# Channel-normalised pixels kept in their natural order: the permutation moves from ScalarE's operands to TensorE's PSUM writes, and one subtraction moves from VectorE to GpSimd

## The reference

```python
corrs = [jnp.sum(x * jax.lax.dynamic_slice(xp, (0, 0, di, dj), (b, c, h, w)), axis=1) for di in range(k) for dj in range(k)]
gs = gs / norm
feat = jnp.concatenate([x, gs], axis=1)
out = jnp.einsum('bchw,oc->bohw', feat, W) + bias[None, :, None, None]
return jax.nn.relu(out)
...
return frac_b * b_out + frac_s * s_out + x
...
x = x + _L0_conv_ref(_gn(x), L0_conv_W, L0_conv_bias)
x = x + _L1_conv_ref(_gn(x), L1_conv_w1, L1_conv_b1, L1_conv_w2, L1_conv_b2)
```

## Time and profile before

| | |
|---|---|
| median of 3 runs | 4609.29 us (4605.99 to 4613.17) |
| the profiled execution | 4614.89 us, its span 4613.1 us |
| TensorE busy | 3847.0 us (83%) |
| VectorE busy | 3520.3 us (76%) |
| ScalarE busy | 2589.7 us (56%) |
| GpSimd busy | 637.1 us (14%) |
| mean granted TensorE clock | 0.928 of full speed |

### The profile page before, as it was taken

How to read it: one execution, slowest core, us unless ns; L and a number is a source line. 1 busy time by engine, 2 the same in 40 slices (tenths; PEclk the granted TensorE clock), 3 DMA queues, 4 the chain that set the end, 5 groups by cost and what they waited for, 6 DMA issues and landing times. The chain is left out here.

```text
span 4613.1 us, 73329 instructions
## 1 busy us (share of the span) xinstructions
PE 3847.0 (83%) x23656; PEld 2135.8 (46%) x23657; DVE 3520.3 (76%) x4010; ACT 2589.7 (56%) x2830; POOL 637.1 (14%) x624
## 2 busy tenths in 40 slices
PE   3999999999999999999989767898888777777665
PEld 2655555555555555555556443343333333323222
DVE  5676667667666765766665576899999999999994
ACT  4777777777777777777777434443333233232322
POOL 0000000000000000000000012333232322222221
PEclk9999999999999999999999878898899888888887
DMA  4233322323333232333321246553333333323221
GB/s 167 97 116 116 109 103 100 134 98 116 116 116 111 99 120 97 116 116 116 115 98 61 61 129 217 180 182 154 146 147 134 132 143 125 134 107 123 111 119 48
DMA packets 174313, 556.98 MB, mean 121 GB/s; under 512 B 91248, under 2 KB 91248, under 8 KB 157552
## 3 DMA queue, kind: packets, MB, share of 16 engines
q1 hardware_dynamic: 152016, 283.62, 17.7%
q0 software_dynamic: 21920, 268.59, 15.1%
HBM read 277.23 MB, written 274.86 MB: 120 GB/s over the span
## 5 line engine op out<-in xcount | busy, mean ns | idle before, releaser
L931 DVE TENSOR_TENSOR arena<-arena 128x2048 f32<-128x2048 f32 (+4 forms) x730 | 1759.1, 2430 | 107.7 <-ACT arena L579 66.3
L1250 PE MATMUL psum<-arena 128*128 128x512 f32 x1072 | 615.0, 658 | 442.0 <-issue 399.0
L1056 PE MATMUL psum<-arena 128*128 128x256 f16 (+1 forms) x6344 | 744.2, 272 | 152.7 <-DVE arena L713 134.8
L579 ACT ACTIVATE arena<-arena 128x4096 f32<-128x4096 f32 x67 | 244.2, 3645 | 972.3 <-DVE arena L931 706.6
L1079 PE MATMUL psum<-arena 128*128 128x512 f16 x2048 | 782.3, 382 | 0.7 <-ACT arena L520 0.7
L1080 PE MATMUL psum<-arena 128*128 128x512 f16 x2048 | 782.3, 382 | 0.0
L1081 PE MATMUL psum<-arena 128*128 128x512 f16 x2048 | 782.1, 382 | 0.0
L520 ACT ACTIVATE arena<-psum,bias_sb 128x512 f32<-128x512 f32 x512 | 577.5, 1184 | 270.6 <-PE psum L1134 171.3
L1056 PEld LDWEIGHTS psum<-arena 128*128 128x128 f16 x6344 | 597.4, 99 | 241.5 <-issue 124.1
L713 DVE TENSOR_TENSOR arena<-arena 128x512 f16<-128x512 f32 x512 | 351.7, 687 | 432.0 <-ACT arena L508 431.9
L506 ACT ACTIVATE arena<-arena,gbias,grstd 128x512 f32 (+1 forms) x512 | 669.3, 1307 | 6.0 <-DVE arena L713 4.7
(11 more groups left out here) (138 smaller groups left out, 2672.0 us busy)
## 6 DMA issues: line engine op xcount, KB each, us to landing
arena<-in_x SPq DMA_DIRECT2D x64, 2048.0 KB, 12.6
y_planes<-arena SPq DMA_DIRECT2D x64, 2048.0 KB, 7.9
arena<-arena SPq DMA_DIRECT2D x1536, 8.0 KB, 1.7
arena<-plane_records,arena POOLq DMA_INDIRECT x67, 3.0
arena<-y_planes,arena POOLq DMA_INDIRECT x67, 9.4
out<-arena POOLq DMA_INDIRECT x67, 8.7
arena<-in_wt SPq DMA_DIRECT2D x1, 1024.0 KB, 12.6
cst<-in_consts SPq DMA_DIRECT2D x1, 768.0 KB, 4.3
```

The source lines that it names most:

```text
L931: ins = dve.tensor_tensor(dst, a, b, ALU.max)
L1056: return pe.matmul(dst, w, m, start=(k == 0), stop=(k == nk - 1))
L1250: pe.matmul(dst, diag[:, s, 0, :], bufs[:, u, b * CW:(b + 1) * CW], start=True, stop=False)
```

## The change

`normalise` reads x and writes `g32` and `gh` in natural order, and `conv_out` reads and writes natural order. All operands of these ScalarE instructions become contiguous. The Gram matmuls take natural-order pixels and put their columns into class order through the access pattern of their PSUM output (`classed`, which now iterates natural order over class-order storage). Consecutive columns are 16 float32 (64 bytes) apart there. The transposes write PSUM through the same pattern. The tail writes into a natural-order convolution bank, with consecutive columns 8 float32 apart instead of in runs of 16 neighbours. The constants `band` and `pick` are adapted, and the partitions of a Gram block are now in natural order. The low parts are formed on GpSimd, after its two small instructions of the same chunk, with the same semaphores. VectorE keeps the statistics of the next image in one piece.

```diff
-        def turned(a):
-            return a.rearrange("p (u r j k) -> p u k r j", r=2, j=8, k=8)
         def classed(a):
-            return a.rearrange("p (u k r j) -> p u k r j", k=8, r=2, j=8)
+            return a.rearrange("p (u k r j) -> p u r j k", k=8, r=2, j=8)
...
         @block.gpsimd
+            def low_parts(i, c):
+                n0 = (i * CH + c) * CT
+                slot = slice((c % RING) * CW, (c % RING + 1) * CW)
+                for ct in range(CT):
+                    pool.wait_ge(s_gh, n0 + ct + 1)
+                    pool.tensor_tensor(gl[:, ct, slot], g32[:, ct % 2, :], gh[:, ct, slot],
+                                       ALU.subtract).then_inc(s_gl, 1)
+            def image(i, last):
                 for c in range(CH):
...
                     pool.tensor_tensor(fl[:, half, :], fn, fh[:, half, :], ALU.subtract).then_inc(s_t, 1)
+                    if c + 3 < CH:
+                        low_parts(i, c + 3)
+                    elif not last:
+                        low_parts(i + 1, c + 3 - CH)
...
-                    piece = turned(xs(ct, c * CW, CW, i % 2))
-                    act.activation(classed(g32[:, ct % 2, :]), piece, ACT.Identity, bias=gbias[:, ct:ct + 1],
+                    piece = xs(ct, c * CW, CW, i % 2)
+                    act.activation(g32[:, ct % 2, :], piece, ACT.Identity, bias=gbias[:, ct:ct + 1],
                                    scale=grstd[:, ct:ct + 1])
-                    act.activation(classed(gh[:, ct, (c % RING) * CW:(c % RING + 1) * CW]), piece, ACT.Identity,
+                    act.activation(gh[:, ct, (c % RING) * CW:(c % RING + 1) * CW], piece, ACT.Identity,
...
-                act.activation(turned(relu[:, o % 2, :]), classed(psum[:, o, :]), ACT.Relu, bias=bias_sb[:, o:o + 1],
+                act.activation(relu[:, o % 2, :], psum[:, o, :], ACT.Relu, bias=bias_sb[:, o:o + 1],
...
-            def low_parts(i, c, stats=None):
-                n0 = (i * CH + c) * CT
-                slot = slice((c % RING) * CW, (c % RING + 1) * CW)
-                for ct in range(CT):
-                    dve.wait_ge(s_gh, n0 + ct + 1)
-                    dve.tensor_tensor(gl[:, ct, slot], g32[:, ct % 2, :], gh[:, ct, slot],
-                                      ALU.subtract).then_inc(s_gl, 1)
-                    if stats:
-                        stats(ct)
...
-                        low_parts(i, c + 3, (lambda ct: x_stats(i + 1, c, ct)) if c < 4 and not last else None)
-                    elif not last:
-                        low_parts(i + 1, c + 3 - CH)
+                    if c < 4 and not last:
+                        for ct in range(CT):
+                            x_stats(i + 1, c, ct)
...
-                        dst = psum[:, GRAM0 + t % 2, col:col + n]
+                        dst = classed(psum[:, GRAM0 + t % 2, col:col + n])
...
-                    last = pe.transpose(psum[:, BANK_N, (t % PAIRS) * P:(t % PAIRS + 1) * P],
+                    last = pe.transpose(classed(psum[:, BANK_N, (t % PAIRS) * P:(t % PAIRS + 1) * P]),
...
-                src = tpair[0:REP, half, :].rearrange("p (t q u s) -> p q u t s", t=QUADS, q=2, u=PAIRS)
+                src = tpair[0:REP, half, :].rearrange("p (t q s) -> p q t s", t=QUADS, q=2)
-                    dst = psum[:, o, :].rearrange("p (u t q s) -> p q u t s", u=PAIRS, t=QUADS, q=2)
+                    dst = psum[:, o, :].rearrange("p (s t q) -> p q t s", t=QUADS, q=2)
```

More of the change, by code:

```diff
@@ L49, in const_arrays @@
     p = np.arange(P)
-    k, r, j = p // 16, p // 8 % 2, p % 8
-    w = 8 * j + k
-    band = (np.abs(w[:, None] - w[None, :]) <= KS // 2).astype(np.float32)
+    w_col = 8 * (p % 8) + p // 16
+    band = (np.abs(p[:, None] % W - w_col[None, :]) <= KS // 2).astype(np.float32)
     pick = np.zeros((P, 3, 2, QUADS, 32), np.float32)
     for role in range(3):
+        r, k = (p // 8 % 2, p // 16) if role == AFTER else (p // W, p % 8)
         for e in range(2):
@@ L400, in _ @@
         def _(pool):
-            def image(i):
+            def low_parts(i, c):
[6 more added lines that the diff above has]
+            def image(i, last):
                 for c in range(CH):
@@ L411, in image @@
                     pool.tensor_tensor(fl[:, half, :], fn, fh[:, half, :], ALU.subtract).then_inc(s_t, 1)
-            image(0)
-            with pool.Fori(1, B) as i:
-                image(i)
+                    if c + 3 < CH:
+                        low_parts(i, c + 3)
+                    elif not last:
+                        low_parts(i + 1, c + 3 - CH)
+            for c in range(3):
+                low_parts(0, c)
+            image(0, False)
+            with pool.Fori(1, B - 1) as i:
+                image(i, False)
+            image(B - 1, True)
             pool.wait_ge(s_conv, B * CH * CT)
@@ L777, in image @@
                         keep_stats(i - 1)
-                    if c + 3 < CH:
-                        low_parts(i, c + 3, (lambda ct: x_stats(i + 1, c, ct)) if c < 4 and not last else None)
-                    elif not last:
-                        low_parts(i + 1, c + 3 - CH)
+                    if c < 4 and not last:
+                        for ct in range(CT):
+                            x_stats(i + 1, c, ct)
                     if c == STATS_AT - 1 and not last:
@@ L1023, in _ @@
             group_values(0)
-            for c in range(3):
-                low_parts(0, c)
             masks_of(0, 0, [[]] * PAIRS)
```

## The result

The changed kernel takes 5152.7 us (5138.5 to 5156.8, median of 4 runs) against 4611.2 us (4606.0 to 4616.5, 4 runs). The ratio is 1.117, with a 95% interval of 1.114 to 1.120. The forecast was 5134 us, slower.

The account below looks back on a forecast made before the run. TensorE was taken to set the pace, losing some 1.9 us per chunk to the chain behind it. 4614.9 - 196 (loop) - 16 (start) + 737 (strided writes) gave 5140, or 5134 us on the median's scale; range 4385 to 5260.

Parts of the forecast that it names:

- Strided PSUM writes cost a factor of two: Layer 0's Gram and tail matmuls: 0.214 us per 256 columns, 0.105 us more each, 737 us in all; chance 0.52.
- ScalarE's doubling: ScalarE's strided operands cost 1308 against 689 ns, about twice; used as the nearest row for strided PSUM writes.
- The sum: Whole kernel: 4403 us after loop and start savings, plus 737 us for strided writes, 5140 us in the profiled execution.
- twice the cost: Own range of the case where strided writes cost a factor of about 1.9 to 2.2: 5080 to 5260 us.
- the free case: Rival 1: strided PSUM writes cost TensorE nothing; 4397 us on the median's scale, chance 0.33.
- The transposes cost nothing more: Transposes on TensorE already run at the halved rate, 0.108 us for 128 columns, so strided writes add nothing.
- The waits of Gram 0 and of the average go: TensorE's waits in layer 0's loop, 121.4 and 26.4 us, vanish; loop with free writes 2331 us in place of 2527.
- the new durations: Twelve ScalarE instructions per chunk, made contiguous, take 0.69 us each, saving 6.9 us per chunk off TensorE's path.
- GpSimd: Each of its four subtractions per chunk takes 1.44 us, bounds 0.69 and 1.71, with no wait left for Gram 0.
- rival 4: GpSimd becomes the bound with writes free, its subtractions slowed beside VectorE; 4842 us at 3.0 us each, chance 0.03.
- the rival's spare time: Spare 1.8 us per chunk before Gram 0, into which waits from GpSimd and VectorE contention would still fit.
- The start: Before layer 0's loop: the first selection starts near 65.5 instead of 81.67, saving 16 us.

Follow-up runs that it names:

- E3: Changed kernel with Gram matmuls writing PSUM in pairs of neighbouring columns, pairs 64 bytes apart (columns at wrong places): 4484.2 us.
- E4: Changed kernel with Gram outputs written with a step of 8 bytes instead of 64 (columns at wrong places): 5137.7 us.
- E9: E3 with the Gram output and the mask's read moved by one float32, so each pair straddles a multiple of 8 bytes: 5138.3 us.
- E10: Changed kernel with each Gram output one contiguous run starting one float32 further, at an odd element (columns at wrong places): 4494.7 us.
- E1: Changed kernel with PSUM outputs of Gram matmuls, transposes and tail all contiguous (columns at wrong places): 4386.9 us.
- E5: Kernel before with only the low-part subtractions moved from VectorE to GpSimd: 4627.4 us, ratio 1.004.
- E2: Changed kernel with contiguous Gram writes, the permutation made by VectorE's mask reading PSUM 32 bytes apart; tail and transposes stay strided: 4498.3 us, ratio 0.976.
- E8: Changed kernel with contiguous Gram writes, the permutation made in the Gram matmul's SBUF read of its moving operand (16 bytes apart): 7000.3 us.

## Why the prediction was right, step by step

- **Strided PSUM writes cost a factor of two: right.** 0.216 us from start to start against 0.214 predicted, 645 + 109 = 754 us against 737. The missing 17 us are in the price of one matmul: it is 0.107 us and not 0.105, and 7016 x 0.107 = 751. The argument was not complete, though. The rows of before gave a bound on either side, and ScalarE's doubling was only an analogy in another memory. Nor was it a doubling. Without their stride the same instructions take 0.804 us in place of 1.308 and 0.686 in place of 1.184, factors of 1.63 and 1.73. So the row that was to decide for two does not say two, and the exact factor was in part luck. E3, E4, E9 and E10 show the rule: a matmul keeps its rate where two columns in a row share an aligned 8 bytes.
- **The sum: closer than its terms.** In the profiled execution 5138.5 us stand against 5140. The loop is 8 us over (3076 against 2331 + 737 = 3068) and the start saves 1 us less than the sum has. What follows the last selection, which the sum left as it was, is 10.6 us shorter, and no run shows why. The range of 5080 to 5260 for twice the cost was said to reach a factor of 2.2. By the prediction's own price it reaches about 2.1. The whole range took in the free case as well, so the experiments confirm the mechanism, not the range.
- **The transposes cost nothing more: right** (0.60 us, 0.60 us).
- **The waits of Gram 0 and of the average go: right.** The loop with free writes was put at 2331 us; E1 measured 2320.
- **The free case as rival: the size was right** (4397 predicted, 4387 in E1), its condition false.
- **ScalarE: the new durations were too low.** The evacuation took 0.686 us (0.69 predicted), but the eight normalising instructions 0.804 us. L599 takes one per-partition operand and reads PSUM, these take two and read SBUF. Which of the two makes the difference no run separates. It is 0.9 us per chunk, hidden behind TensorE.
- **GpSimd: 1.30 us** (1.44 predicted, bounds 0.69 and 1.71), and 1.16 us on average in E5. The contention of rival 4 exists. In E2 VectorE's residual L745 takes 1.27 us beside L404, against 0.69 without it:

```profile
1318.31 1.16 POOL L404 TENSOR_TENSOR arena<-arena 128x512 f16<-128x512 f32 x1 [4.88 <-ACT arena L521]
1318.75 1.27 DVE L745 TENSOR_TENSOR arena<-arena 128x512 f32 x1
```

  It stayed off the path, as the rival's spare time said. The Trainium skill's "SBUF — State Buffer", section Who interferes with whom, says that a VectorE instruction with two SBUF inputs contends with a GpSimd instruction that reads SBUF, and these rows agree.
- **The start: 14.9 us of 16.** One reason given was wrong. I assumed that the first Gram matmuls would run at half clock and so keep their rate with strided writes. They do start slowly, and they do not keep their rate:

```profile
52.32 4.65 PE L1054 MATMUL psum<-arena 128*128 128x256 f16 x11 [10.08 <-POOL arena L404]
56.76 8.19 PE L1054 MATMUL psum<-arena 128*128 128x256 f16 x37
```

  The first eleven are (56.76 - 52.32) / 11 = 0.40 us apart, the next 37 0.216 us. In the kernel before, the first ones were 0.21 us apart. (The profile's clock record starts only at 56.6 us, so the slow clock before it is read from the pace.) E8 says the same: at a granted clock of 0.50 the strided tail has a distance of (3.59 - 0.70) / 7 = 0.41 us, against 0.214 for contiguous writes. The price is a factor of two at either clock. In E2, where the Gram writes are contiguous, the first selection starts at 62.7 us, so the strided writes cost the start 4 us. The forecast of 65.5 us left them out and was near because the rest of the start was quicker than its estimate.

Not tried: a tail without its stride. Its two halves fill alternate columns, so it would need another pixel order, worth the 109 us that E3 and E1 differ by.

## What to carry to other kernels

A permutation is not free because it is put into an access pattern, and its price depends on whose pattern: 645 us as TensorE's PSUM write, 2493 us as TensorE's SBUF read (the loops of E8 and E2), nothing as VectorE's float32 read of PSUM (E2). Before a stride goes onto the engine that sets the pace, compare the distance of its instructions with and without it, and let two neighbouring float32 columns share each aligned 8 bytes of a matmul's output. If a move takes away every wait of an engine and the kernel is slower, look at the distance between that engine's own instructions first.

## What the runs showed of the hardware that I had not expected

- The price of a strided PSUM write does not vanish at half clock: 0.41 us for 256 columns at a granted clock of 0.50 (E8's tail), 0.216 at 1.00.
- A moving operand of float16 columns 16 bytes apart took 0.45 us per 256 columns at a granted clock of 1.00 and of 0.50 alike. The clock fell to 0.50 in that work although TensorE had no gaps (E8, mean 0.735).
- VectorE reads float32 from PSUM with a step of 32 bytes in 415 ns where a contiguous read took 412 to 425 ns (before, E3, the changed kernel).
- The alignment counts, not the neighbourhood: the same pairs of columns cost 4484 us from an even and 5138 us from an odd element.
